# Recurrent convolution and mixture layer on one core: tanh before the forget sigmoid, the cell state in a PSUM bank, turns in halves, a reordered setup

## The reference, cut to what matters

```python
x = x + conv_ref(_ln_c(x))        # 1: recurrence over the 32 rows
t = tokens(x)                     # (16, 1024, 64)
t = t + ffn_ref(_ln_t(t))         # 2: experts that choose their tokens
# 1
def step(carry, f_j):             # f_j: convolution of the normalised input, row j and the row above
    h, c = carry
    pre = conv(h, w_stos) + b_stos + f_j
    i, g, f, o = split(pre, 4)
    c_new = sigmoid(f) * c + sigmoid(i) * tanh(g)
    h_new = c * sigmoid(o)        # the OLD c
    return (h_new, c_new), h_new
# 2
logits = x_norm @ gate_w.T + gate_b     # 32 experts
# softmax over the 1024 tokens, the best 8 tokens of each expert, pooled,
# two dense layers per expert, the result added back to those tokens
```

## Time and profile before

| | |
|---|---|
| median of 3 runs | 217.4 us (216.65 to 219.28) |
| the profiled execution | 219.67 us |
| its span, first to last instruction | 217.9 us |
| mean granted TensorE clock | 0.968 |
| busy: TensorE, VectorE, GpSimd, ScalarE | 83%, 76%, 57%, 51% of the span |

### The profile page before, as it was taken

One profiled execution on the slowest core, in us unless ns is written; L12 is line 12 of the kernel. 1 busy time (PEld: TensorE's weight loads), 2 busy tenths in 40 slices (PEclk: granted clock), 3 DMA queues, 4 the chain that ended last, 5 costly groups with the idle time before them and its releaser, 6 DMA issues.

```text
span 217.9 us, 10845 instructions
## 1 busy us (share of the span) xinstructions
...
## 2 busy tenths in 40 slices
...
DMA packets 28640, 19.12 MB, mean 88 GB/s; under 512 B 2240, under 2 KB 27568, under 8 KB 28592
## 3 DMA queue, kind: packets, MB, share of 16 engines
...
## 4 chain that ended last, share of the span: by engine, by line
PE 59%; DVE 20%; issue 8%; POOL 5%; DMA 2%; ACT 2%; DVEq 0%; POOLq 0%
PE ps L918 42%; PE ps L909 9%; PE ps L975 3%; DVE ig L691 3%; DMA xc<-in_x 2%; DVE tail_room L902 2%; DVE xtok L902 2%; DVE x_split L843 2%; ACT ps L490 2%; DVE cell L695 2%; POOL r L387 2%; DVE st L647 2%; DVE ps L687 1%; POOL rb_xr L354 1%; DVE lg L848 1%
## 5 line engine op out<-in xcount | busy, mean ns | idle before, releaser
L918 PE MATMUL ps<-x_split,w_hi 64*64 64x256 f16 x1000 | 51.1, 277 | 8.5 <-DVE cell L695 3.3
L918 PEld LDWEIGHTS ps<-x_split,w_hi 64*64 64x64 f16 x1000 | 26.5, 109 | 19.9 <-issue 11.2
L347 POOL TENSOR_TENSOR xc<-xc,h 128x256 f32<-128x256 f32 x31 | 22.5, 726 | 30.0 <-DVE h_lo L673 29.7
L474 ACT ACTIVATE ps<-ps,bias 128x256 f32<-128x256 f32 x32 | 14.3, 448 | 42.2 <-PE ps L918 42.2
L918 PE MATMUL ps<-h_lo,w_hi 64*64 64x256 f16 x750 | 33.6, 277 | 1.1 <-issue 1.0
L918 PE MATMUL ps<-h_hi,w_lo 64*64 64x256 f16 x750 | 33.2, 276 | 0.5 <-issue 0.5
L918 PE MATMUL ps<-h_hi,w_hi 64*64 64x256 f16 x750 | 32.6, 276 | 0.0
L691 DVE TENSOR_TENSOR ig<-sg_i,ps 64x256 f32<-64x256 f32 x62 | 26.0, 419 | 1.9
L369 POOL TENSOR_TENSOR r<-v,pow_exp 128x16 f32<-128x16 f32 x7 | 20.5, 2934 | 9.5 <-DVE v L641 9.5
L918 PE MATMUL ps<-x_split,w_lo 64*64 64x256 f16 x500 | 25.3, 276 | 0.0
L909 PE MATMUL ps<-ident,xc 128*128 128x128 f32 x128 | 18.3, 288 | 7.7 <-DMA xc<-in_x 6.2
...
## 6 DMA issues: line engine op xcount, KB each, us to landing
rb_xr<-scratch SPq DMA_DIRECT2D x14, 256.0 KB, 5.5
xc<-in_x ACTq DMA_DIRECT2D x9, 256.0 KB, 3.9
...
xc<-in_x SPq DMA_DIRECT2D x7, 256.0 KB, 4.3
rbf<-scratch SPq DMA_DIRECT2D x24, 64.0 KB, 4.1
out<-tail_room SPq DMA_DIRECT2D x4, 256.0 KB, 4.5
out<-tail_room ACTq DMA_DIRECT2D x4, 256.0 KB, 4.9
```

The source lines that it names most:

```text
L347: p.tensor_tensor(here, here, h32[:, i % 2, :].rearrange("p (b w) -> p b w", w=W), ALU.add) \
L474: a.activation(pre[O][:, 0:COLS], pre[O][:, 0:COLS], ACT.Sigmoid, bias=bias[:, 3:4]).then_inc(s_sg_o, 1)
L918: ins = pe.matmul(pre[gate][to, 0:COLS], w[half(h), tap, C * GATE_ORDER[gate]:][:, 0:C], data[half(h)], start=first and m == 0, stop=s_don ...
```

## The change

- **Setup.** The x of group 0 is loaded in halves with semaphores of their own, and each half is turned as it lands. GpSimd makes the first `h_lo`, VectorE copies the first cell. VectorE takes the input's weight taps first. TensorE starts the first rows when `x_hi` and four `w_lo` are there, and waits for `x_lo` after 16 products; `rows_of_x` does so at every later even row too.
- **Step.** Sigmoids of O and F go to SBUF (`sg_o`, `sg_f`). ScalarE takes tanh(G) before sigmoid(F). The cell lies alone in bank 5. `new_cell` does the two products with tanh first, then F * cell, then the sum. TensorE waits for `s_sg_f` and `s_ig` before the rows of F and G, and for `s_sg_o` instead of `s_h32` before those of O and I.
- **Turns.** Bank 5 being taken, both turns go through bank 4 in halves of 4, each half at a place of its own: `turn_x1` in `between(t,0)` and `inside(t,1)`, `turn_in` in `between(t,2)` and `between(t,3)`. On VectorE all statistics stand in `after`, 8 at a time.
- **Logits.** Eight products of 64x32, 256 columns, into the first halves of banks 6 and 7. r0 and r1 are turned into the second half of bank 7, so these turns also wait until the last logits are scaled (`s_scaled_logits`). In group 0 `turn_r0(2)` moves from `inside(0,2)` to `inside(0,3)`, and its `variances0(2)` from step 1 to step 2.
- **Loads.** `load_later` moves from ScalarE's queue to SyncE's, behind the spreads.
- **Tail.** Other banks; the last products go by image instead of by pair; `keep_logits(7)` stands before `row_expert`.

```diff
+        psum = [... (f"ps{i}", [128, 512], F32) for i in range(6)]
+        ps_end = ...psum_tensor("ps_end", [128, 2, 512], F32)
+        ps_turn = psum[4], psum[4]
+        cell = psum[5][:, 0:COLS]
+        ps_lg, ps_r = ps_end[:, :, 0:2 * TOK], psum[7][:, 256:]
...
 @block.gpsimd
-            p.tensor_copy(cell[:, 0, :]...)
+            p.wait_ge(s_h_hi, 1)
+            p.tensor_tensor(h_lo[0]..., h_first..., h_hi[0]..., ALU.subtract)
                 residual(t, 0)
                 if t == 0:
+                    residual(0, 1)
                     rsqrt0(2)
-                    residual(0, 1)
                     scale_rows(1, 0)
+                    residual(0, 2)
+                    lo_of_x(1, 0)
                     scale_rows(1, 1)
...
 @block.scalar   step(n)
-                a.activation(pre[O]..., pre[O]..., ACT.Sigmoid, bias=bias[:, 3:4])
+                wait(a, s_h32, n)
+                a.activation(sg_o[:, :], pre[O]..., ACT.Sigmoid, bias=bias[:, 3:4])
...
+                if n == 1:
+                    keep_r0t(1)
                 a.wait_ge(s_h32, n + 1)
                 hi_part(par, 1 - par)
-                if n == 1:
-                    keep_r0t(1)
...
-                a.activation(pre[F]..., pre[F]..., ACT.Sigmoid, bias=bias[:, 2:3])
+                if i == 1 and t > 0:
+                    keep_tokens(t - 1, 1)
                 a.activation(pre[G]..., pre[G]..., ACT.Tanh, bias=bias[:, 1:2])
+                wait(a, s_fc, n)
+                a.activation(sg_f[:, :], pre[F]..., ACT.Sigmoid, bias=bias[:, 2:3])
...
 @block.vector   new_cell(n)
-                v.tensor_tensor(pre[F]..., pre[F]..., cell[:, par, :], ALU.mult)
                 for h in range(2):
                     v.tensor_tensor(ig[half(h), :], sg_i[half(1 - h), :], pre[G]..., ALU.mult)
+                v.tensor_tensor(cell, sg_f[:, :], cell, ALU.mult)
-                v.tensor_tensor(cell[:, 1 - par, :], pre[F]..., ig[:, :], ALU.add)
+                v.tensor_tensor(cell, cell, ig[:, :], ALU.add)
...
 between(t, i)
-                if i == 1 and t > 0:
-                    stats1(t - 1, 8, 12)
-                if i == 3 and u < NT:
-                    stats0(u, ps_t, 1, 0, 4)
 after(t, i)
-                    stats1(t - 1, 12, 16)
+                    stats1(t - 1, 8, 16)
-                    stats0(u, ps_t, 1, 4, 8)
+                    stats0(u, ps_turn, 1)
...
 @block.tensor
-                    ins = pe.matmul(ps_lg[C * j:C * j + C, :], gw[:, :], xc[:, j::2, u, :], ...)
+                for q in range(QUAD):
+                    for a in range(2):
+                        ins = pe.matmul(ps_lg[E * q:E * q + E, a, :], gw[half(a), :], xc[half(a), q::QUAD, u, :], ...)
...
                     turn_r1(t - 2)
-                if i == 2 and t + 2 < NT:
+                if i == 2 and 0 < t and t + 2 < NT:
...
+                    wait(pe, s_scaled_logits, t - 1)
                     turn_r0(t + 2)
...
-                    pe.wait_ge(s_cell, n)
+                    pe.wait_ge(s_sg_f, n)
+                    pe.wait_ge(s_ig, 2 * n)
...
-                pe.wait_ge(s_h32, n + 1)
+                pe.wait_ge(s_sg_o, n + 1)
```

301 lines of the change are left out of this document (159 added, 142 removed).

## The result

| | before | after |
|---|---|---|
| median, 7 runs each | 218.7 us (216.65 to 221.96) | 223.5 us (221.35 to 228.9) |
| ratio after / before | | 1.021, 95% interval 1.015 to 1.028 |
| profiled execution, its span | 219.67, 217.9 | 228.9, 227.0 |
| mean granted TensorE clock | 0.968 | 0.952 |

The change costs 2.1%; forecast was 212.7, a gain. H(n) is again the start of `new_state` of step n, and a stretch is a time in which TensorE stands idle.

A forecast was written before the change was run, and what follows sets the result against it. It took latency to bound the kernel up to 39.78 us, then a nearly full TensorE. Terms -6.2 (to H(4)), +1.9 (groups 1 to 3), -0.4 (groups 4 to 7), 0 (tail) gave -4.7: 212.7 us, range 209.5 to 216.8.

The forecast's parts named there:

- minus 6.2: Setup and row group 0: earlier x, first rows and r0(1) copy put H(4) at 37.3, 6.2 us earlier.
- (a): Setup: two half loads of x let the powers start 1.3 us earlier, bounds 0 to 1.4; weights have similar slack.
- plus 0.8: Row group 1: late r0(2) leaves TensorE idle 2.5 us before step 6; 18.3 us against 17.5.
- store 1.5; loads land at 41.8: Row group 1: r0t(2), copied after sigmoid F of step 3 at 35.1, is stored in 1.5 us; loads land at 41.8.
- rival 1: Clock or start: longer idle before step 6 drops the clock, or weights come later; 214.4 us with both; chance 0.22.
- plus 0.7 each: Full row groups 2, 3 and 4: each takes 19.0 us against 18.28 before.
- It loses 1.1: Full row groups: VectorE loses 1.1 us because the r0 turn in step i = 2 waits for the scaled logits.
- Halved turns: Full row groups: four-tile turns cost 0.6 us where eight cost 1.02, so 0.35 us more a group.
- I add 0.2, since VectorE's slack hides more of them: Full row groups: 0.2 us added to the 18.8 sum for short gaps inside streams of products, giving 19.0.
- Edits at nothing: Sigmoids into SBUF, cell in PSUM, SyncE loads and tail were put at 0; tail bounds -0.6 and +0.5 us.
- Rival 3: Logit scaling waits for late `rbf` on SyncE's shared queue: up to +9, 221.7 us, half gives 217 to 218; chance 0.1.
- Rival 4: Loop eats the start: groups at 19.5, group 1 stall at full length, 216.2 us; chance 0.08.

The follow-up runs named there:

- e4: Changed kernel with the later loads of x and expert weights issued by ScalarE again instead of SyncE; 229.8 us, 1.043 of the kernel before.
- e6: Changed kernel with r0 of groups 3 to 7 in gate F's bank, r0(2) copied inside step 3, later loads on ScalarE; 221.3 us, 1.018 of before.
- f2: Kernel before with its eight expert weight loads issued by SyncE behind the last row group; 214.3 us, 0.987 of the kernel before.
- f4: Kernel before with one line added: the r0 turn in step i = 2 waits for the scaled logits; 220.3 us, 1.012 of the kernel before.
- e1: Changed kernel with x of group 0 loaded whole again instead of in halves; 223.6 us, 1.030 of the kernel before.
- a0: Changed kernel run again without any edit; 223.2 us, 1.024 of the kernel before.
- e5: Changed kernel with r0 of groups 3 to 7 turned into gate F's bank, without the wait for scaled logits; 220.3 us, 0.999 of the kernel before.
- e8: Changed kernel with r0 of groups 3 to 7 in gate F's bank and expert weight loads behind the last group's spread; 218.5 us, 1.002 of before.
- g3: Changed kernel with the eight expert weight loads behind the last row group; 225.7 us, 1.018 of the kernel before.
- e3: Changed kernel with r0(2) copied inside step 3 and x of group 4 loaded by ScalarE behind step 0; 223.3 us, 1.028 of the kernel before.
- e7: Changed kernel with r0(2) prepared, turned and copied a step earlier, x(2) turned in one go; 222.2 us, 1.010 of the kernel before.
- e2: Changed kernel with the r0 turn and its copy moved from step i = 2 to i = 3 in groups 1 to 5; 226.8 us, 1.040 of before.

## Why the prediction was wrong, step by step

The order of events came as forecast; the sizes did not. The terms of the sum, and the same terms between the two first profiles:

| term | forecast | measured |
|---|---|---|
| to H(4) | -6.2 | -2.8 |
| groups 1 to 3 | +1.9 | +7.6 |
| groups 4 to 7 | -0.4 | +3.7 |
| tail | 0 | +0.7 |
| sum | -4.7 | +9.1 |

The medians are 4.8 apart, since the profile of after shows a long execution; what follows therefore uses the other profiles too. Three terms failed: the start was half of the forecast, the store and landing of r0(2) were longer, and the full groups lost 0.5 to 0.8 more each. A fourth was put at nothing, the fall of the clock in the loop.

**Setup, "minus 6.2": came to about 3.** The chain was right: the power of r0(2) binds. H(0) to H(4) took 20.2 in all eight profiles with this group 0 and SyncE's loads (21.1 and 20.8 with ScalarE's, e4 and e6), where the forecast's own marks have 18.9 (H(1) = 22.5, so H(0) near 18.4). What was missing is behind the split: its end at 35.12 to H(4) is 5.6, not 4.7, and the power starts 1.0 behind H(2) and takes 3.1. As large an error was the other end of the difference: H(4) of before, 43.47, was the latest of three profiles of that setup (41.97 in f2, 40.12 in f4; mean 41.9). With the changed group 0 eight profiles lie from 37.2 to 40.7, mean 38.8. I took one draw of a landing for a constant.

**Setup, (a), "x in halves".** The weights did have less slack than I wrote (the chain of after starts with `w_rows`, landed at 9.3, not with x), but e1 shows no difference in time.

**Row group 1, "plus 0.8".** The step that failed is "store 1.5; loads land at 41.8": the store took 3.5 here and 2.6 to 3.5, 3.1 in the mean, in the six profiles with this group 1 (after, a0, e1, e5, e8, g3), with no load issued shortly ahead; from the loads' issue to the product passed 5.2 to 7.2, 6.1 in the mean, where 5.1 was taken. So the stretch of 2.5 became 1.9 to 4.5, and the low clock, rival 1, came in all of the six but e5, which has the shortest stretch. Their mean is 21.2, against 17.5: plus 3.7. Why the store is slow at this place stays open. By H(8) the start is spent: mean 60.4 there, 59.4 in the three profiles of the old order.

**Full row groups, "plus 0.7 each".** "It loses 1.1" was right: 1.0 (g3 against e8). Halved turns were mis-sized: a stream of 60 products with a turn behind it takes 1.78 to 1.81 and one without 1.68, so four visits of 0.59 and 0.10 to 0.13 stand against two of 1.02 and 0.10: 0.5 to 0.6 more a group, not 0.35. The logits were right, 0.60 against 1.01 in f2. The term that failed most is "I add 0.2, since VectorE's slack hides more of them": the sum for before, 17.75, fell 0.5 short of the trace (0.3 of it are stops, by f2), and that for after, 18.8, fell 0.7 to 1.0 short. Of the 0.49 between a full group of e8 and one of f2, these two explain 0.1 to 0.2 (half turns less logits); the rest was not traced. Measured 19.5 to 19.8 for 19.0.

**The clock in full groups, not forecast.** A stretch of 2.0 before an r0 turn lost the clock once in most profiles of the changed loop (group 4 of after, a0 and e3, group 5 of e1; twice in e7, groups 2 and 4; never in e4 and g3): 21.05 against 19.78, so 1.3, and 1.6 in e1. I had looked for it only at step 6.

**Groups 5 to 7.** 17.9, 18.6 and 13.5 (to the last `new_state`) for 17.5, 17.6 and 12.9. The first two fall to 16.95 and 17.88 in e8, the third to 13.3, so 0.4 stays in group 7; what takes it was not looked into.

**Edits at nothing: right but for the tail.** Sigmoids of O into SBUF take 473 ns where they took 448. The tail, from the last `new_state` on, took 53.3 for 52.6, just over the bound of 0.5; the clock fell in it, behind the stretch of 2.2 before the last turn of x (1.5 in before and in e3, which took 52.4). Rival 3 (`rbf` late) did not come with the change, only in e2.

**Rivals.** Rival 4 (the loop eats the start, groups at 19.5, group 1 at full length) is what happened, with rival 1 on top; I gave it 216.2 and a chance of 0.08, since it too started from the 6.2. The slower side beyond my range, which ended at 216.8, was priced on `rbf` alone.
